# Moving the Wq preparation into the first feed-forward phase and regrouping buffers and statistics in a macaron transformer layer

## The chip, the cores and the metric

The kernel runs on one Trainium2 chip, on all eight of its cores. Every core runs the same program on its own two sequences of the batch of sixteen, and no core waits for another. The metric is the device time of the slowest core, in microseconds (us). The engines of a core are named as the profile names them: PE is TensorE's matrix multiply, PEld its weight load, DVE is VectorE, ACT is ScalarE, POOL is GpSimd and SP is SyncE. SP and POOL here do little but issue DMAs; a "q" behind an engine's name is its queue of such issues.

## The reference

The layer is a feed-forward half step, attention, and a second feed-forward half step, each ahead of a residual sum. Cut to what matters:

```python
def ln(x):  return (x - mean(x)) / sqrt(var(x) + 1e-5)      # over 1024
def ffn(x): return (silu(x @ wg.T) * (x @ wu.T)) @ wd.T     # hidden 3072, int weights / 127
def attn(x):                                                # 16 heads of 64
    xn = ln(x) * ln_g + ln_b
    q, k, v = xn @ Wq + bq, xn @ Wk + bk, xn @ Wv + bv
    return softmax(q @ k.T / 8, over the keys) @ v

x = x + 0.5 * ffn(ln(x))      # x: [16, 2048, 1024] float32
x = x + attn(x)
x = x + 0.5 * ffn(ln(x))
```

Weights are random, `ln_g` is ones and `ln_b` zeros, but the kernel computes with all of them.

## The kernel before, in words

**Phases.** The program is a chain of phases, and each phase is a block: no engine starts the next one before all engines and the phase's DMAs are done (`flush` waits for the DMAs). First two preparation phases turn the integer weights into bf16 and transpose them into DRAM. Then come, for each of the two sequences `s`, four phases: `a1` (first feed-forward, `ffn_phase`, input x, result in the DRAM tensor `x1s`), `a2` (`qkv_phase`: Q, K and V of the whole sequence, kept in SBUF), `att` (`attn_phase`, result in the DRAM tensor `x2s`) and `c` (second feed-forward, `ffn_phase` again, with `ext_stats=True`). Within a phase each engine executes its instructions strictly in the order in which the code emits them; `deps` become semaphore waits. So the order of the work is the order of the Python loops, engine by engine.

**ffn_phase.** The 2048 rows are 16 tiles `tt` of 128 rows, in two groups `g` of eight. For a group, SP loads the tiles (L379, L388), DVE sums each (L395), ACT sums its squares (L398), and after four tiles `stats_chain` (L194 to L212) turns the sums into mean and reciprocal deviation by a short ping-pong of ACT and DVE. Then, tile by tile, DVE normalises into `xntm` (L422), PE transposes (L435), DVE evacuates into `xnfm` (L444). Then 48 blocks of 16 gate and up matmuls (L483, L489) with SiLU on ACT (L500) and the product on DVE (L506); the weight slabs are loaded two ahead by SP (L461, L465). Then 16 blocks of 24 down matmuls (L527), each followed by the residual sum on DVE (L545); POOL stores a finished tile (L554). Tiles 0 to 11 use eight slots `xst`, so that tiles 8 to 11 wait until tiles 0 to 3 are summed at L545; tiles 12 to 15 have a buffer of their own, `xst2`. Phase `c` does not compute the statistics of tiles 0 to 11: the attention phase left their sums in `sm2_s` and `sm2_q`, and three chains at the phase's start finish them. It computes those of tiles 12 to 15 itself, between the two groups.

**qkv_phase.** POOL loads Wq, Wk and Wv with a cast to bf16, eight DMAs each (L582). For each of the three PE multiplies the bias of the layer norm into it (L597, 16 matmuls), DVE adds the bias vector (L607) and scales the weight by `ln_g`, the "fold" (L615, 8 instructions). Then four groups `g4` of four tiles: load (L647), sums (L652 on DVE, L655 on ACT), chain, normalise (L669), transpose (L682), evacuate (L694); 8 blocks each of Q and K (8 matmuls L714 and a bias matmul L720, evacuated at L738 through two PSUM banks) and 8 of V (L756, L762, L771).

**attn_phase.** For each of four query groups `qg` and eight head pairs `hp`: 16 rounds of two score matmuls (L960) and one exponential on ACT (L974), with the matmuls of the probabilities and V (L869) of the head pair before in between. Twice per head pair DVE normalises the result into `x2b` (L892, L897, L902), and PE may not reuse the PSUM banks before that. After the first head pair of the next query group, `drain_qg` sums four tiles of the old one with x1 (L923) and POOL stores them (L929). x1 comes into `x1q`, which holds two tiles: the load for tiles 2 and 3 (L917) waits for the first two sums, and DVE waits for this load. Later `stats_push` computes on DVE, for query groups 0 to 2, the sums that phase `c` uses (L937, L941, L944).

The lines of the phases' main loops can be followed below; the statistics chain and `drain_qg` are where the order of DVE decides.

Of the kernel before, what the change touches and what calls it, by code (L numbers as in the profile page):

```python
# [7 lines left out]
F32 = mybir.dt.float32  # L8
BF16 = mybir.dt.bfloat16
# [7 lines left out]
D = 1024  # L17
# [18 lines left out]
class Phase:  # L36
# [26 lines left out]
    def op(self, eng, fn, deps=(), inc=None, n=1, pre_nops=0, pre_drain=False,  # L63
           fdeps=()):
# [11 lines left out]
        for t in fdeps:  # L76
            if t is None:
                continue
            sem, val, ep, src = t
            if ep < p.epoch:  # L80
                continue
            wl.append((sem, val))
            if val > p.waited.get((eng, sem), -1):
                p.waited[(eng, sem)] = val
            waits.pop(sem, None) if waits.get(sem, -1) <= val else None
# [36 lines left out]
def build_program(debug=False, stages=("prep", "a1", "a2", "norm", "b", "c")):  # L122
# [51 lines left out]
    sm2_s = SB("sm2_s", [128, 16], F32)  # L174
    sm2_q = SB("sm2_q", [128, 16], F32)
    sm2_m = SB("sm2_m", [128, 16], F32)
    sm2_r = SB("sm2_r", [128, 16], F32)
# [16 lines left out]
    def stats_chain(ph, b, t_red, t_sq, prev_done, bufs=None):  # L194
        ss, qq, mm_, rr = bufs if bufs else (sm_s, sm_q, sm_m, sm_r)
        c0, c1 = b * 4, b * 4 + 4
        deps = [t_red[b * 4 + i] for i in range(4)] if t_red else []
        t_m = ph.op("scalar", lambda e: e.mul(mm_[:, c0:c1], ss[:, c0:c1], 1.0 / D),  # L198
                    deps=deps + ([prev_done] if t_red is None else []), inc="sc")
        t_m2 = ph.op("scalar", lambda e: e.activation(  # L200
            sm_t1[:, c0:c1], mm_[:, c0:c1], AF.Square),
            deps=[prev_done, t_m], inc="sc")
        t_var = ph.op("vector", lambda e: e.scalar_tensor_tensor(
            out=sm_t2[:, c0:c1], in0=qq[:, c0:c1], scalar=1.0 / D,
            in1=sm_t1[:, c0:c1], op0=ALU.mult, op1=ALU.subtract),
            deps=[t_m2] + ([t_sq[b * 4 + i] for i in range(4)] if t_sq else []),
            inc="ev")
# [4 lines left out]
            rr[:, c0:c1], sm_t1[:, c0:c1]), deps=[t_sd], inc="ev")  # L212
# [111 lines left out]
    def ffn_phase(name, src_ap, dst_ap, with_prep=False, ext_stats=False):  # L324
# [8 lines left out]
        with (  # L333
            nc.sbuf_tensor(name + "_xst", [128, nslots * 1024], F32) as xst,
            nc.sbuf_tensor(name + "_xs2", [128, 4 * 1024], F32) as xst2,
            nc.sbuf_tensor(name + "_xntm", [128, 4 * 1024], BF16) as xntm,
# [30 lines left out]
            if ext_stats:  # L367
                for b_ in range(3):
                    t_statsdone[b_] = stats_chain(
                        ph, b_, None, None,  # L370
                        t_statsdone[b_ - 1] if b_ >= 1 else None,
                        bufs=(sm2_s, sm2_q, sm2_m, sm2_r))

            for g in range(2):
                for ti in range(8):
                    tt = g * 8 + ti
                    slot = tt % nslots
                    if tt < 12:
                        t_load[tt] = ph.op("sync", lambda e, tt=tt, slot=slot: e.dma_start(  # L379
                            xst[:, slot * 1024:(slot + 1) * 1024],  # L380
                            src_ap[tt * 128:(tt + 1) * 128, :]),
                            deps=([t_xn[tt - 8],
                                   None if ext_stats else t_sq[tt - 8],
                                   t_stt.get((0, tt - 8, 1))]
                                  if tt >= 8 else []),
                            inc=ph.ld(f"x{slot}"), n=16)
                    else:
                        t_load[tt] = ph.op("sync", lambda e, tt=tt: e.dma_start(  # L388
                            xst2[:, (tt - 12) * 1024:(tt - 11) * 1024],
                            src_ap[tt * 128:(tt + 1) * 128, :]),  # L390
                            inc=ph.ld(f"y{tt - 12}"), n=16)
                    xs_ = xst2 if tt >= 12 else xst
                    xo_ = (tt - 12 if tt >= 12 else slot) * 1024
                    if not ext_stats or tt >= 12:
                        t_red[tt] = ph.op("vector", lambda e, tt=tt, xs_=xs_, xo_=xo_: e.reduce_sum(  # L395
                            sm_s[:, tt:tt + 1], xs_[:, xo_:xo_ + 1024],
                            axis=AX.X), deps=[t_load[tt]], inc="ev")
                        t_sq[tt] = ph.op("scalar", lambda e, tt=tt, xs_=xs_, xo_=xo_: e.activation(  # L398
                            sqscr[:], xs_[:, xo_:xo_ + 1024], AF.Square,
                            accum_out=sm_q[:, tt:tt + 1]),  # L400
                            deps=[t_load[tt],
                                  t_sq[tt - 1]
                                  if (tt >= 1 and (not ext_stats or tt >= 13))
                                  else None],
                            inc="sc")
                        if tt % 4 == 3:
                            b_ = tt // 4
# [713 lines left out]
```

How the kernel before makes its waits and increments, by code:

```python
                def body(e, ops=ops, eng_name=eng_name):  # L108
                    for fn, wl, inc, n, pre_nops, pre_drain in ops:
                        for sem, val in wl:
                            e.wait_ge(p.sems[sem], val)
                        if pre_drain:
                            e.drain()
                        inst = fn(e)
                        if inc is not None:
                            inst.then_inc(p.sems[inc], n)
# [5 lines left out]
def build_program(debug=False, stages=("prep", "a1", "a2", "norm", "b", "c")):  # L122
# [63 lines left out]
    def flush(ph):  # L186
        for lane in list(ph._ld.values()):
            ph.op("sync", lambda e, l=lane: e.wait_ge(sems[l], P.C[l]))
        for lane in list(ph._st.values()):
            ph.op("gpsimd", lambda e, l=lane: e.wait_ge(sems[l], P.C[l]))
        for lane in list(ph._sd.values()):
            ph.op("scalar", lambda e, l=lane: e.wait_ge(sems[l], P.C[l]))
# [893 lines left out]
                    qkv_phase(s, K_sb, Q_sb, V_sb)  # L1086
                if "b" in stages:
                    attn_phase(s, K_sb, Q_sb, V_sb)
        if "c" in stages:
            ffn_phase(f"cs{s}", x2s.ap(), out_d.ap()[s], ext_stats=True)
        if "one_seq" in stages:
            break
    ph = Phase(P, "fin")
    for i in range(8):
        ph.op("gpsimd", lambda e, l=f"st{i}": e.wait_ge(sems[l], P.C[l]))
    ph.run()
    es.close()
```

## Time and profile before

| what | value |
|---|---|
| runs of the kernel | 4415.39, 4552.08, 4901.65 us (median 4552.08) |
| the profiled execution's own time | 4441.22 us |
| its span, slowest core (core 5) | 4439.5 us; the eight cores 4383.5 to 4439.5 us |
| PE busy, share of the span | 3485.7 us, 79% |
| ACT busy | 1393.2 us, 31% |
| DVE busy | 1099.7 us, 25% |
| POOL busy | 142.8 us, 3% |
| mean granted TensorE clock, eight cores | 0.900 to 0.916 of full speed |

Shares are means over phases with different limits, so the table does not say what an edit is worth; the phases have to be read one by one. The views used are the busy time of each engine by stretch, the timeline (start in us from the span's start, duration in us, engine, line, instruction, count, and in brackets how long the engine was idle just before and who released it), the list of waits, and the list of DMA issues with the median time from issue to landing.

### The profile page before, as it was taken

To read this page: it belongs to the slowest core of one execution; us is meant where nothing else is said; L and a number is where in the kernel's file an instruction comes from. 1 tells how busy PE (TensorE), PEld (TensorE's weight loads), DVE (VectorE), ACT (ScalarE), POOL (GpSimd) and SP (SyncE) were. 2 spreads that over 40 slices of the span, in tenths; PEclk is the share of its full clock that TensorE was granted. 3 is DMA by queue.
4 is the path that set the end of the run, shared out by engine and by line. 5 is a ranking of instruction groups with operands and counts; after the bars stand their busy time and mean duration, and the time that the engine had idled before them with its cause. 6 is when DMAs were issued, how large, how long until landed. Compare 5 with 4: busy or idle time off the path is not lost. (4 is left out here: it accounts for less than half of the span.)

```text
span 4439.5 us, 57373 instructions; the slowest of 8 cores (4383.5 to 4439.5 us)
## 1 busy us (share of the span) xinstructions
PE 3485.7 (79%) x22790; PEld 1660.6 (37%) x22790; DVE 1099.7 (25%) x1734; ACT 1393.2 (31%) x1650; POOL 142.8 (3%) x267
## 2 busy tenths in 40 slices
PE   3379889678776666898996979958777676599899
PEld 2234344223233333343443434423224343344344
DVE  3421221133402212212113122123330222221221
ACT  0021111000199997111102111000029999611110
POOL 2200000100000000000000000010000000000000
PEclk9988989888889998898998989978889888899899
DMA  7933321510001110332213432150000111123220
GB/s 238 284 85 90 120 57 48 114 38 10 10 1 39 39 39 30 105 116 94 76 43 95 119 95 67 48 119 24 10 10 1 39 39 39 68 76 123 86 76 38
DMA packets 264787, 316.21 MB, mean 71 GB/s; under 512 B 9032, under 2 KB 205640, under 8 KB 263504
## 3 DMA queue, kind: packets, MB, share of 16 engines
q1 hardware_dynamic: 238288, 230.74, 17.8%
q0 software_dynamic: 26240, 81.80, 6.0%
q8 instruction: 188, 3.08, 0.3%
q14 instruction: 71, 0.58, 0.0%
HBM read 255.89 MB, written 69.21 MB: 73 GB/s over the span
## 5 line engine op out<-in xcount | busy, mean ns | idle before, releaser
L974 ACT ACTIVATE att_eS<-PS,cb 128x1024 bf16<-128x1024 f32 x1024 | 1035.2, 1190 | 47.5 <-PE PS L960 47.2
L960 PE MATMUL PS<-Q,K 64*128 64x512 bf16 x2048 | 436.3, 418 | 290.8 <-ACT att_eS L974 280.1
L869 PE MATMUL PS<-V,att_eS 128*128 128x65 bf16 x8192 | 372.4, 203 | 38.8 <-DVE att_x2b L902 38.2
L483 PE MATMUL PS<-a1s_xnfm,a1s_wslg 128*128 128x512 bf16 x1536 | 384.9, 396 | 0.0
L489 PE MATMUL PS<-a1s_xnfm,a1s_wslu 128*128 128x512 bf16 x1536 | 380.0, 392 | 0.0
L869 PEld LDWEIGHTS PS<-V,att_eS 128*128 128x128 bf16 x8192 | 309.4, 103 | 172.2 <-issue 172.2
L483 PE MATMUL PS<-cs_xnfm,cs_wslg 128*128 128x512 bf16 x1536 | 369.1, 384 | 0.0
L489 PE MATMUL PS<-cs_xnfm,cs_wslu 128*128 128x512 bf16 x1536 | 364.2, 380 | 0.0
L527 PE MATMUL PS<-cs_wdsb,cs_hsb 128*128 128x512 bf16 x1536 | 332.2, 379 | 7.5 <-DVE cs_hsb L506 7.5
L527 PE MATMUL PS<-a1s_wdsb,a1s_hsb 128*128 128x512 bf16 x1536 | 332.2, 379 | 7.5 <-DVE a1s_hsb L506 7.5
L960 PEld LDWEIGHTS PS<-Q,K 64*128 64x128 bf16 x2048 | 125.6, 94 | 492.0 <-issue 437.8
L500 ACT ACTIVATE a1s_sg<-PS 128x512 bf16<-128x512 f32 x192 | 114.6, 597 | 563.8 <-PE PS L489 563.8
L500 ACT ACTIVATE cs_sg<-PS 128x512 bf16<-128x512 f32 x192 | 114.7, 597 | 532.3 <-PE PS L489 532.3
L506 DVE TENSOR_TENSOR a1s_hsb<-PS,a1s_sg 128x512 bf16<-128x512 f32 x192 | 132.8, 692 | 571.9 <-ACT a1s_sg L500 571.9
L506 DVE TENSOR_TENSOR cs_hsb<-PS,cs_sg 128x512 bf16<-128x512 f32 x192 | 132.8, 692 | 541.1 <-ACT cs_sg L500 541.1
L483 PEld LDWEIGHTS PS<-a1s_xnfm,a1s_wslg 128*128 128x128 bf16 x1536 | 155.4, 101 | 196.4 <-issue 59.0
L489 PEld LDWEIGHTS PS<-a1s_xnfm,a1s_wslu 128*128 128x128 bf16 x1536 | 154.2, 100 | 194.4 <-issue 54.0
L892 DVE TENSOR_SCALAR att_lb<-PS 128x4 f32<-128x4 f32 x128 | 20.7, 162 | 812.9 <-PE PS L869 801.5
L527 PEld LDWEIGHTS PS<-cs_wdsb,cs_hsb 128*128 128x128 bf16 x1536 | 150.0, 98 | 189.6 <-issue 9.3
L527 PEld LDWEIGHTS PS<-a1s_wdsb,a1s_hsb 128*128 128x128 bf16 x1536 | 150.0, 98 | 189.6 <-issue 9.3
L483 PEld LDWEIGHTS PS<-cs_xnfm,cs_wslg 128*128 128x128 bf16 x1536 | 151.8, 99 | 184.1 <-issue 6.7
L489 PEld LDWEIGHTS PS<-cs_xnfm,cs_wslu 128*128 128x128 bf16 x1536 | 150.7, 98 | 183.1 <-issue 3.3
(119 smaller groups left out, 2133.7 us busy)
## 6 DMA issues: line engine op xcount, KB each, us to landing
a1s_wslg<-wgT SPq DMA_DIRECT2D x48, 512.0 KB, 4.1
a1s_wslu<-wuT SPq DMA_DIRECT2D x48, 512.0 KB, 5.4
cs_wslg<-wgT SPq DMA_DIRECT2D x48, 512.0 KB, 4.1
cs_wslu<-wuT SPq DMA_DIRECT2D x48, 512.0 KB, 5.4
x1s<-a1s_xo POOLq DMA_DIRECT2D x32, 512.0 KB, 3.0
a2s_xst<-x1s SPq DMA_DIRECT2D x32, 512.0 KB, 3.9
att_x1q<-x1s SPq DMA_DIRECT2D x16, 1024.0 KB
x2s<-att_x2o POOLq DMA_DIRECT2D x32, 512.0 KB, 4.8
```

What stands on the lines that cost most here:

```text
L483: e.matmul(gview, lg, rhs, start=(dc == 0), stop=(dc == 7))
L489: inst = e.matmul(uview, lu, rhs, start=(dc == 0), stop=(dc == 7))
L500: "scalar", lambda e, gview=gview, th=th: e.activation(sgb[:, (th % 2) * 512:(th % 2 + 1) * 512], gview, AF.Silu),
L506: "vector", lambda e, uview=uview, hc=hc, th=th: e.tensor_mul(hsb[:, hc * 1024 + th * 512: hc * 1024 + (th + 1) * 512], uview, sgb[:, (th ...
L527: inst = e.matmul(dview, hsb[:, hc * 1024 + ti * 128: hc * 1024 + (ti + 1) * 128], wdsb[:, hc * 1024 + oh * 512: hc * 1024 + (oh + 1) * 51 ...
L869: inst = e.matmul(PS1[:, (par * 2 + q2) * 512: (par * 2 + q2) * 512 + 65], expS[:, buf + kt * 1024 + par * 512 + qt * 128: buf + kt * 1024 ...
L892: t_l = ph.op("vector", lambda e, qtp=qtp: e.tensor_scalar(out=lbuf[:, qtp * 4: qtp * 4 + 4][:, :, None], in0=PS1[:, :].rearrange("p (a t) ...
L960: inst = e.matmul(PS0[:, pp + par * 512: pp + (par + 1) * 512], K_sb[64 * par:64 * par + 64, hp * 2048 + r * 128: hp * 2048 + (r + 1) * 12 ...
L974: "scalar", lambda e, hp=hp, r=r, buf=buf, pp=pp: e.activation(expS[:, buf + r * 1024: buf + (r + 1) * 1024], PS0[:, pp:pp + 1024], AF.Exp ...
```

## The change

The change has four parts. It renumbers the lines: a line L of the kernel after stands some 10 to 45 lower than its counterpart.

1. **Statistics of phase c.** `sm2_*`, `ext_stats`, `stats_push` and their three DVE instructions per tile go. Phase `c` sums all its tiles itself, as `a1` does.
2. **Buffers of ffn_phase.** `xst2` goes; tiles 12 to 15 use the eight slots and wait for tiles 4 to 7 at the residual sum. `xntm` has two buffers for four. The slabs of gate and up get semaphores of their own.
3. **Wq.** The load, bias product and fold of Wq move from `a2` to the end of `a1`, emitted behind all of a1's other work, into a buffer `wq_s` that outlives the phases. `a2` prepares Wk and Wv only. Waits for the folds are put where each weight is first used.
4. **Order in a2, buffers in att.** In `a2` the sums and the chain of group `g4+1` are emitted after the evacuations of group `g4`'s transposes, ahead of its Q, K and V. In `att`, `nsq` and `x2o` lie in `wq_s` (free by then), `x2o` has two tiles for four, and `x1q` has four tiles for two and is loaded once per query group.

```diff
@@ ffn_phase, per tile (slots are 8, tt from 0 to 15) @@
-                    if tt < 12: ... deps t_stt.get((0, tt - 8, 1)) if tt >= 8 ...
-                    else: t_load[tt] = ... xst2[...]          # no wait
-                    if not ext_stats or tt >= 12:
+                    t_load[tt] = ph.op("sync", ... xst[:, slot * 1024:(slot + 1) * 1024] ...,
+                        deps=([t_xn[tt - nslots], t_sq[tt - nslots],
+                               t_stt.get(((tt - nslots) // 8, (tt - nslots) % 8, 1))]
+                              if tt >= nslots else []),
                         t_red[tt] = ... reduce_sum
                         t_sq[tt] = ... Square
-            if ext_stats:
-                for b_ in range(3):
-                    t_statsdone[b_] = stats_chain(ph, b_, None, None, ..., bufs=(sm2_s, sm2_q, sm2_m, sm2_r))
@@ ffn_phase, after both groups (a1 only) @@
+            if wprep2 is not None:
+                wq_s, bbq = wprep2
+                for dc in range(8):
+                    wcast[dc] = ph.op("gpsimd", ... dma_start(wq_s[:, dc * 1024:(dc + 1) * 1024],
+                            Wq_d.ap()[dc * 128:(dc + 1) * 128, :]), inc=ph.st(f"w{dc % 2}"), n=16)
+                t_lb = ph.op("gpsimd", ... dma_start(bbq[0:1, :], bq_d ...))
+                t_bm = ph.op("tensor", bmm, deps=[wcast[dc] for dc in range(8)] + [t_ev[14], t_ev[15]], inc="mm")
+                ph.op("vector", ... tensor_add(bbq[0:1, :], PS0[0:1, 0:1024], bbq[0:1, :]), deps=[t_bm, t_lb])
+                for dc in range(8):
+                    ph.op("vector", ... tensor_scalar_mul(wq_s[...], wq_s[...], gch[:, dc:dc + 1]), deps=[t_bm])
             flush(ph)
@@ qkv_phase @@
-            for wi, (wsrc, wdst) in enumerate(((Wq_d, Wqs), (Wk_d, Wks), (Wv_d, Wvs))):
+            for wi, wsrc, wdst in ((1, Wk_d, Wks), (2, Wv_d, Wvs)):
...
+            emit_stats_a2(0)
             for g4 in range(4):
-                (load, sums and chain of group g4)
                 (normalise, transpose, evacuate the four tiles of g4)
+                if g4 < 3:
+                    emit_stats_a2(g4 + 1)
                 (Q, K and V of g4)
@@ attn_phase @@
+        nsq = wq_s[:, 0:4096]
+        x2o = wq_s[:, 4096:8192].bitcast(F32)
-            nc.sbuf_tensor(nm + "_x1q", [128, 2 * 1024], F32) as x1q,
+            nc.sbuf_tensor(nm + "_x1q", [128, 4 * 1024], F32) as x1q,
             def drain_qg(qg):
                 for qt in range(4):
-                    if qt == 2:
-                        t_x1[(qg, 1)] = ph.op("sync", ... x1q <- x1s tiles 2 and 3, deps=[t_x2add[(qg, 1)]])
                     t_x2add[(qg, qt)] = ph.op("vector", ... x2o = x2b + x1q,
-                        deps=[t_yev[(qg, 7, qt // 2)], t_x1[(qg, qt // 2)],
-                              t_store.get(fi - 4), t_st2.get(fi - 4)], inc="ev")
+                        deps=[t_yev[(qg, 7, qt // 2)], t_x1[qg],
+                              t_store.get(fi - 2)], inc="ev")
                     t_store[fi] = ph.op("gpsimd", ... x2s <- x2o ...)
-                    if qg >= 1 and qg - 1 < 3 and hp in (1, 2, 3, 4):
-                        stats_push(qg - 1, hp - 1)
```

How this moves the instructions, at the three places that the prediction speaks of. POOL's queue around the border of `a1` and `a2`, before (a row is one instruction or, with xN, a run of N):

```order
L554 DMA x1s<-a1s_xo 128x1024 x16
L102 UNCONDITIONAL_BRANCH
L118 UNCONDITIONAL_BRANCH
L582 DMA a2s_Wq<-L_attn_Wq 128x1024 x8
L582 DMA a2s_Wk<-L_attn_Wk 128x1024 x8
L582 DMA a2s_Wv<-L_attn_Wv 128x1024 x8
```

The same place after (`Wqh` is the buffer `wq_s`; the two branches are the border of the phases):

```order
L508 DMA x1s<-a1s_xo 128x1024 x16
L519 DMA Wqh<-L_attn_Wq 128x1024 x8
L523 DMA bbq<-L_attn_bq 1x16x64
L91 UNCONDITIONAL_BRANCH
L107 UNCONDITIONAL_BRANCH
L572 DMA a2s_Wk<-L_attn_Wk 128x1024 x8
```

The loads of Wq have moved over the border, and in POOL's queue they stand behind all 16 stores of `a1`.

DVE in `a2` from the last evacuation of group 0's transposes to the first normalisation of group 1, before (`sm_s` are the sums, `Q`, `K`, `V` the evacuations of the matmuls):

```order
L694 COPY a2s_xnfm<-PS 128x8x128
L738 CAST Q<-PS 128x512 x8
L738 CAST K<-PS 128x512 x8
L771 CAST V<-PS 128x8x64 x8
L652 TENSOR_REDUCE sm_s<-a2s_xst 128x1 x4
L203 SCALAR_TENSOR_TENSOR sm_t<-sm_q,sm_t 128x4
L211 RECIPROCAL sm_r<-sm_t 128x4
L669 TENSOR_SCALAR a2s_xntm<-a2s_xst,sm_m,sm_r 128x1024
```

The same place after:

```order
L686 COPY a2s_xnfm<-PS 128x8x128
L642 TENSOR_REDUCE sm_s<-a2s_xst 128x1 x4
L187 SCALAR_TENSOR_TENSOR sm_t<-sm_q,sm_t 128x4
L194 RECIPROCAL sm_r<-sm_t 128x4
L734 CAST Q<-PS 128x512 x8
L734 CAST K<-PS 128x512 x8
L770 CAST V<-PS 128x8x64 x8
L661 TENSOR_SCALAR a2s_xntm<-a2s_xst,sm_m,sm_r 128x1024
```

The four sums and the chain have moved from behind the 24 evacuations to ahead of them.

SP's queue in the attention phase, before (one row for each load of `x1q` until the third query group):

```order
L948 DMA att_x1q<-x1s 128x2x1024
L917 DMA att_x1q<-x1s 128x2x1024
L987 DMA att_x1q<-x1s 128x2x1024
L917 DMA att_x1q<-x1s 128x2x1024
L987 DMA att_x1q<-x1s 128x2x1024
```

The same queue after, for all four query groups:

```order
L925 DMA att_x1q<-x1s 128x4x1024
L962 DMA att_x1q<-x1s 128x4x1024 x3
```

The loads in the middle of a drain (L917) are gone; each remaining load has four tiles.

## Rows read from the trace of the kernel before

**Rows 1.** Stretches c, a1: length, PE, PEld, DVE, ACT, POOL busy, clock, DMA, GB/s

```profile
1776.00:2342.00 566.00, 517.57 (x2432) 238.53 (x2432) 117.17 (x172) 69.92 (x120) 8.52 (x16) 0.95 0.28 86
2342.00:2926.00 584.00, 516.40 (x2432) 238.32 (x2432) 130.96 (x184) 83.34 (x144) 8.52 (x16) 0.93 0.28 83
```

**Rows 2.** Timeline, start of c (sequence 0), then start of a1 (sequence 1)

```profile
1776.34 4.04 SPq L379 DMA_DIRECT2D cs_xst<-x2s  x8
...
1783.10 1.01 PE L435 MATMUL PS<-ident,cs_xntm 128*128 128x128 bf16 x8 [25.67 <-DVE cs_xntm L422]
...
2342.93 4.52 SPq L379 DMA_DIRECT2D a1s_xst<-L_attn_x  x8
...
2362.25 1.01 PE L435 MATMUL PS<-ident,a1s_xntm 128*128 128x128 bf16 x8 [25.29 <-DVE a1s_xntm L422]
```

**Rows 3.** Timeline between the two groups, in c (sequence 0), then in a1 (sequence 1)

```profile
2065.23 1.01 PE L435 MATMUL PS<-ident,cs_xntm 128*128 128x128 bf16 x8 [9.07 <-DVE cs_xntm L422]
...
2642.11 4.60 DVE L395 TENSOR_REDUCE sm_s<-a1s_xs 128x1 f32<-128x1024 f32 x4
...
2649.13 1.01 PE L435 MATMUL PS<-ident,a1s_xntm 128*128 128x128 bf16 x8 [15.06 <-DVE a1s_xntm L422]
```

**Rows 4.** DMA issues: line, count, KB each, median us from issue to landing

```profile
x1s<-a1s_xo POOLq DMA_DIRECT2D x32, 512.0 KB, 3.0
a2s_xst<-x1s SPq DMA_DIRECT2D x32, 512.0 KB, 3.9
...
x2s<-att_x2o POOLq DMA_DIRECT2D x32, 512.0 KB, 4.8
```

**Rows 5.** Timeline, border of a1 and a2, sequence 0

```profile
834.53 0.26 SPq L591 DMA_DIRECT2D a2s_bvec<-L_attn_bq  x1
835.01 4.25 POOL L582 DMA_DIRECT2D a2s_Wq<-L_attn_Wq  x8 [4.83 <-POOLq L102]
...
852.70 4.95 PE L597 MATMUL PS<-a2s_Wq,bchb 128*1 128x512 bf16 x16 [24.38 <-DMA a2s_Wq<-L_attn_Wq]
...
858.97 3.24 DVE L615 TENSOR_SCALAR a2s_Wq<-a2s_Wq,gch 128x1024 bf16<-128x1024 bf16 x8
...
864.81 5.71 PE L597 MATMUL PS<-a2s_Wk,bchb 128*1 128x512 bf16 x16 [7.16 <-DMA a2s_Wk<-L_attn_Wk]
```

**Rows 6.** Timeline of a2, sequence 0: first Q evacuation of group 0, then group 1's start

```profile
909.93 0.69 DVE L738 CAST Q<-PS 128x512 bf16<-128x512 f32 x1 [4.36 <-PE PS L720]
...
960.11 4.59 DVE L652 TENSOR_REDUCE sm_s<-a2s_xst 128x1 f32<-128x1024 f32 x4
...
966.06 0.18 DVE L211 RECIPROCAL sm_r<-sm_t 128x4 f32<-128x4 f32 x1 [0.49 <-ACT sm_t L208]
...
967.30 1.01 PE L682 MATMUL PS<-ident,a2s_xntm 128*128 128x128 bf16 x8 [7.90 <-DVE a2s_xntm L669]
...
969.98 1.01 PE L682 MATMUL PS<-ident,a2s_xntm 128*128 128x128 bf16 x8 [1.67 <-DVE a2s_xntm L669]
```

**Rows 7.** Timeline, first drain in att (sequence 0); last row: sixth stall (sequence 1)

```profile
1359.26 2.35 DVE L923 TENSOR_TENSOR att_x2o<-att_x2b,att_x1q 128x1024 f32<-128x1024 bf16 x2
...
1361.05 0.54 POOL L929 DMA_DIRECT2D x2s<-att_x2o  x1 [512.10 <-DVE att_x2o L923]
...
1373.84 3.12 ACT L974 ACTIVATE att_eS<-PS,cb 128x1024 bf16<-128x1024 f32 x3 [4.69 <-PE PS L960]
...
3742.52 4.13 ACT L974 ACTIVATE att_eS<-PS,cb 128x1024 bf16<-128x1024 f32 x4 [5.52 <-PE PS L960]
```

**Rows 8.** Waits over the whole span: us in total, times, longest us

```profile
DVE att_x2o L923 <- DMA att_x1q<-x1s: 63.6, 8, 9.6
...
ACT att_eS L974 <- PE PS L960: 47.2, 49, 7.1
```

**Rows 9.** Busy time by stretch: gate and up matmuls of group 0 in both a1

```profile
256.00:428.00 172.00, 172.00 (x653) 71.21 (x651) 28.05 (x41) 25.17 (x41) 0.00 (x0) 0.82 0.20 56
...
2382.00:2555.00 173.00, 171.07 (x787) 77.12 (x786) 33.89 (x49) 29.94 (x49) 0.00 (x0) 0.99 0.33 98
```

More of the change, by code:

```diff
@@ L75, in op @@
         wl = []
[L76 to L85, printed above, removed]
         for sem, val in waits.items():
@@ L558, in ffn_phase, with bmm @@
                         inc=ph.st(f"o{ti % 2}"), n=16)
+            if wprep2 is not None:
+                wq_s, bbq = wprep2
+                wcast = {}
+                for dc in range(8):
+                    wcast[dc] = ph.op(
+                        "gpsimd", lambda e, dc=dc: e.dma_start(
+                            wq_s[:, dc * 1024:(dc + 1) * 1024],
+                            Wq_d.ap()[dc * 128:(dc + 1) * 128, :]),
+                        inc=ph.st(f"w{dc % 2}"), n=16)
+                t_lb = ph.op("gpsimd", lambda e: e.dma_start(
+                    bbq[0:1, :], bq_d.ap().rearrange("(a d) -> a d", a=1)),
+                    inc=ph.st("bv"), n=16)
+                def bmm(e):
+                    for oi in range(2):
+                        for dc in range(8):
+                            inst = e.matmul(
+                                PS0[0:1, oi * 512:(oi + 1) * 512],
+                                bchb[:, dc:dc + 1],
+                                wq_s[:, dc * 1024 + oi * 512:
+                                     dc * 1024 + (oi + 1) * 512],
+                                start=(dc == 0), stop=(dc == 7))
+                    return inst
+                t_bm = ph.op("tensor", bmm,
+                             deps=[wcast[dc] for dc in range(8)]
+                             + [t_ev[14], t_ev[15]],
+                             inc="mm")
+                ph.op("vector", lambda e: e.tensor_add(
+                    bbq[0:1, :], PS0[0:1, 0:1024], bbq[0:1, :]),
+                    deps=[t_bm, t_lb], inc="ev")
+                for dc in range(8):
+                    ph.op("vector", lambda e, dc=dc: e.tensor_scalar_mul(
+                        wq_s[:, dc * 1024:(dc + 1) * 1024],
+                        wq_s[:, dc * 1024:(dc + 1) * 1024],
+                        gch[:, dc:dc + 1]),
+                        deps=[t_bm], inc="ev", pre_nops=1)
             flush(ph)
@@ L641, in qkv_phase, with emit_stats_a2 @@
             t_ve = {}
-            for g4 in range(4):
+            def emit_stats_a2(g4):
                 for ti in range(4):
@@ L664, in qkv_phase @@
                             t_statsdone[b_ - 1] if b_ >= 1 else None)
+            emit_stats_a2(0)
+            for g4 in range(4):
                 for ti in range(4):
@@ L847, in attn_phase @@
             t_store = {}
-            t_st2 = {}
             t_exp = {}
@@ L1068, in build_program @@
     for s in range(NSEQ):
+        es2 = ExitStack()
+        wq_s = bbq = None
+        if {"a2", "b"} & set(stages):
+            wq_s = es2.enter_context(nc.sbuf_tensor(f"Wqh{s}", [128, 8 * 1024], BF16))
+            bbq = es2.enter_context(nc.sbuf_tensor(f"bbq{s}", [1, 1024], BF16))
         if "a1" in stages:
-            ffn_phase(f"a1s{s}", x_d.ap()[s], x1s.ap())
+            ffn_phase(f"a1s{s}", x_d.ap()[s], x1s.ap(),
+                      wprep2=((wq_s, bbq) if wq_s is not None else None))
             if debug and s == 0:
```

238 lines of the change are left out of this document (92 added, 146 removed).

## The prediction

> **What bounds the kernel now.** I read the busy time by stretch first, phase by phase, because the shares of the whole span mix four kinds of phase. The reader is to see that the two feed-forward phases do the same matmuls (2432 in each, 517.57 and 516.40 us of PE) and still differ by 18 us, 566 against 584 [rows 1]: DVE and ACT are busier in `a1`, and that work stands where PE waits. So PE bounds these phases, and the ends of the matmul runs are where an edit counts. Then I read the timeline at every place where PE starts again after a pause: the bracket behind a transpose tells how long PE stood [rows 2, 3, 5, 6]. In the attention phase ACT bounds: its exponentials follow each other without a gap but for 49 waits of 47.2 us together [rows 8], and six long ones (4.30 to 7.12 us, 32.6 together, the first and the last shown) come just after the drains, when DVE has waited for x1 [rows 7, 8]. Last comes the list of issues, for what a transfer takes when it is alone [rows 4].
>
> **The change part by part.** All terms are for the whole run: two sequences, the two alike unless I say so.
>
> *Statistics in c: +37.1.* Phase `c` gets the start of `a1`. From SP's first load to the first transpose `c` takes 1783.10 − 1776.34 = 6.76 us, `a1` 2362.25 − 2342.93 = 19.32 [rows 2]; that is 12.56 more. Between the groups PE stands 9.07 us in `c` and 15.06 in `a1` [rows 3], 5.99 more. Twice 18.55 is 37.1, and the two lengths in [rows 1] (18 apart) say the same. Bounds: 33, if the loads of x2 land a little sooner than those of x, and 40. The DVE work taken out of the attention phase (`stats_push`) gives nothing back: ACT is the bound there, and its long waits are not at that place.
>
> *Buffers in ffn: 0.* The loads of tiles 12 to 15 now wait for tiles 4 to 7. The last can be issued when the last residual sum is done: PE ended at 2649.13 − 15.06 = 2634.07, the sum 0.7 later. A load alone lands 3.9 us after its issue [rows 4], at about 2638.8; DVE begins the sums of tiles 12 to 15 at 2642.11 [rows 3]. So what hides it is the four sums and the chain of tiles 8 to 11, by 3 us. The first two slabs of the second group are issued behind that load, but the first gate matmul comes only after eight transposes. If the cover were gone it would cost under 4 us at each of four places. Two `xntm` buffers suffice, because DVE alternates normalisation and evacuation and so is never a tile ahead; semaphores apart for the slabs add a wait that is long satisfied.
>
> *Wq at the end of a1: +47.7.* The loads are not hidden: in POOL's queue they stand behind all the stores, and the last store waits for the last residual sum. POOL was free of it at 835.01 − 4.83 = 830.18. From the first issue of Wq to its bias matmuls `a2` takes 852.70 − 835.01 = 17.69, and from there to the end of the fold 858.97 + 3.24 − 852.70 = 9.51 [rows 5]. So `a1`'s work ends at 830.18 + 17.69 + 9.51 = 857.4; for the border I take 1 us (bounds 0 and 1.9, which is 4.35 from 830.18 to 834.53 less the rest of a store that lands after 3.0 [rows 4]). The next phase starts at 858.4 where it started at 834.53: 23.85 late, 47.7 in all. Upper bound 49.5; lower bound 36.5, if Wq alone, with no Wk and Wv behind it in the queue, lands in the 12.11 us that Wk took after Wq.
>
> By the Trainium skill (DMA: Bandwidth & Descriptors, Specifications and Anatomy of one DMA), a core draws about 358 GB/s from HBM and a DMA has about 2.0 us of fixed cost; its estimate for the 4.19 MB of Wq is 13.7 us, against 17.69 in the row. By that estimate the sum would be 8 us lower, 4419.
>
> *a2 without Wq: −24.2.* The step from Wq's to Wk's bias matmuls, 864.81 − 852.70 = 12.11 [rows 5], falls away; Wk takes Wq's place and Wv that of Wk. Bounds: −24.2, and −16 if the loads of x1, which now start beside more of Wv's load, delay it by about one load's 3.9 us.
>
> *Order in a2: −34.4.* At each of three group borders PE stands 7.90 us before the first transpose, 1.67 before the next one [rows 6]. With sums and chain done, the first has what the next has: 6.23 gained. In exchange the sums stand before the Q evacuations. DVE is free at 909.93 − 4.36 = 905.57, sums take 4.59, the chain 966.24 − 964.70 = 1.54, so the first Q evacuation starts at 911.70 for 909.93, 1.77 late [rows 6]. PE meanwhile fills the second bank, so I take 0.5 of it (bounds 0 and 1.77). Six borders: −6 × 5.73. Bounds −37.4 and −26.8. The tiles' loads are hidden, as the slots that they wait for are normalised before; what is late next is the chain of normalise, transpose and evacuate, which stays.
>
> *Drains in att: −40.1.* DVE's eight waits for x1 (63.6 us, 7.95 each [rows 8]) go, as x1 of all four tiles is there before. In their place the third sum waits for the store of the first. That store is issued at 1361.05, 0.56 before the second sum ends at 1361.61 [rows 7]. A store lands after 3.0 us where nothing runs beside it and after 4.8 in this phase, where the 1 MB loads of x1 do [rows 4]. I take 3.5, nearer the lone one, since two stores are under way; the wait is then 2.94, and 63.6 − 8 × 2.94 = 40.1. The fourth sum finds its store landed. Bounds: −29.7 with 4.8; −43 with 3.0, where the six stalls of ACT are used up and only the two last drains, at the phase's end, give all. Behind the waiting sum on DVE stands the normalisation that PE and so ACT wait for, as before.
>
> **Sum.** 37.1 + 47.7 − 24.2 − 34.4 − 40.1 = −13.9. The profiled execution took 4441.2 us, its span 4439.5; so 4427 us. With all ends of one kind it is 4406 or 4458. The profiled time is 2.4% below the median of the runs shown (4552.08); set on that median the same sum would be 4538. A measurement of this kernel can tell about 2% (89 us) from no change.
>
> **The rivals.**
>
> *The store wait takes the load wait's place.* For it: third and fourth sum need stores to DRAM that are issued only 1.7 us before. If each wait stays 7.95 the drains give nothing: 4427 + 40 = 4467. Against it: 3.0 and 4.8 in [rows 4].
>
> *The sums ahead of Q hold PE up by what they save,* because a sum finds its tile not yet landed. Then a2's order gives nothing: 4461. Against it: the last load of a group waits for a normalisation about 7 us ahead of its sum, and lands in 3.9 [rows 4].
>
> *The change does what it seems to be for, and Wq is hidden in a1:* POOL's issues would start ahead of the last stores. Only bias matmuls, fold and border stay, about 4 us for each sequence instead of 23.85: 4388. Against it is POOL's order.
>
> *Slower, by the clock.* In the first `a1`, the gate and up matmuls of group 0 ran at a granted clock of 0.82, between the two levels, and 653 of them took 172.00 us; in the second, at 0.99, the upper level, 787 took 173.00 [rows 9]: 0.263 and 0.220 us each, 33.5 us for the 768 of a group. If the longer pauses in `c` make its four groups start like that first one, 134 us come on top: 4561. Over 2% it is only with all four; three give 4528. Against it: the second `a1` came out of pauses of 25.29 and 15.06 us [rows 2, 3], what `c` gets, and ran at 0.99.
>
> By the Trainium skill (TensorE: Matmul & The Clock Gate, Part 1, Seeing it yourself), a peak-current limit takes a die to 13/16 of the clock once three of its cores run dense matmuls. The 0.82 agrees with that figure; that all later groups on eight cores ran at 0.99 does not.
>
> **How the numbers follow.** Forecast 0.72, store wait 0.10, sums ahead of Q 0.07, hidden Wq 0.04, slower clock 0.05; 0.02 for a gain of over 2% that I cannot name. The predicted time is the forecast's, 4427. Its own bounds, 4406 to 4458, take in the ends of the unknown costs; the range runs from 4390, near the hidden Wq, to 4530, so that the first two rivals and a clock lowered in up to three groups lie inside. Faster by over 2% would be under 4352: 0.02. Slower by over 2% needs the clock: 0.05. The rest, 0.93, is within 2%.
>
> **What would show it.** Right: PE's first transpose in `c` about 19 us after SP's first load, and about 15 us of standing between the groups; the first issue of Wq right behind the last store of `a1`, its bias matmuls some 17 us later with PE idle all that time; `a2`'s first transpose about 12 us nearer to the phase's start; 1.7 us instead of 7.9 ahead of the first transpose of groups 1 to 3, with the first Q evacuation 1.8 us later; DVE waiting some 3 us for a store in each drain, and ACT's six stalls nearly gone. Wrong: a first `c` matmul stretch with a clock near 0.8, a drain wait near 8 us, sums in `a2` that wait for a load, or Wq landing while down matmuls still run.

## The result, and the profile after

| | before | after |
|---|---|---|
| median of 13 runs each | 4415.39 us | 4388.61 us |
| ratio, 95% interval | | 0.9933, 0.9915 to 0.9951 |
| the profiled execution's span, slowest core | 4439.5 us | 4381.3 us |

The change saves 0.67%, some 30 us (22 to 38), which is within 2%. The forecast was a saving of 13.9 us and a time of 4427; 4388.6 lies just below the range, which began at 4390. Single runs reach 4902 us before and 4796 us after, since some executions are disturbed; the ratio leaves those out, a median does not.

I read the trace phase by phase, on each of the eight cores, from one event of PE to the next. The table has the median over the cores of each piece between two events, summed over both sequences; "again" is a second profile of the same kernel (told of below). The first row is made of two pieces, cut at Wq's first bias matmul. With the border taken in one piece its four medians are 105.7, 107.8, 125.8 and 126.2, a change of 20.1 for the first pair of profiles and 18.4 for the second, so this row is known to some 2 us.

| PE, from ... to ... (us, both sequences) | before | again | after | again | change | forecast |
|---|---|---|---|---|---|---|
| a1's last down matmul to the end of Wv's bias product | 107.8 | 106.4 | 124.3 | 126.1 | +16.5 | +23.5 |
| a2, first transpose to last V matmul | 557.8 | 557.6 | 517.2 | 516.8 | −40.6 | −34.4 |
| from there to the first scores | 71.2 | 71.2 | 69.6 | 70.6 | −1.5 | 0 |
| att, first scores to last probability matmul | 1096.9 | 1096.7 | 1066.0 | 1063.6 | −30.9 | } |
| from there to c's first transpose | 50.9 | 50.5 | 64.6 | 64.3 | +13.7 | } −3.0 |
| c, standing between the groups | 18.1 | 18.1 | 30.2 | 30.2 | +12.0 | } |

The sum is −30.8; all other stretches together changed by under 1 us. So the time of the phases and the timed ratio agree, and the trace tells where the 30 us are.

Now the places of the prediction. The timeline of the kernel after, slowest core (core 6): start, duration, engine, line, and in brackets the idle time before and its releaser.

```profile
798.58 0.53 POOL L508 DMA_DIRECT2D x1s<-a1s_xo  x1 [9.83 <-DVE a1s_xo L498]
799.10 4.26 POOL L519 DMA_DIRECT2D Wqh<-L_attn_Wq  x8
...
817.93 5.06 PE L530 MATMUL PS<-Wqh,bchb 128*1 128x512 bf16 x16 [20.69 <-DMA Wqh<-L_attn_Wq]
...
828.27 4.26 POOL L572 DMA_DIRECT2D a2s_Wk<-L_attn_Wk  x8 [24.40 <-POOLq L91]
...
875.73 1.01 PE L674 MATMUL PS<-ident,a2s_xntm 128*128 128x128 bf16 x8 [11.66 <-DVE a2s_xntm L661]
...
885.48 4.59 DVE L642 TENSOR_REDUCE sm_s<-a2s_xst 128x1 f32<-128x1024 f32 x4
...
891.53 1.29 DVE L734 CAST Q<-PS 128x512 bf16<-128x512 f32 x2
...
941.38 0.61 PE L674 MATMUL PS<-ident,a2s_xntm 128*128 128x128 bf16 x8 [1.67 <-DVE a2s_xntm L661]
...
1321.34 2.35 DVE L914 TENSOR_TENSOR Wqh<-att_x2b,att_x1q 128x1024 f32<-128x1024 bf16 x2
...
1327.48 1.23 DVE L914 TENSOR_TENSOR Wqh<-att_x2b,att_x1q 128x1024 f32<-128x1024 bf16 x1 [3.80 <-DMA x2s<-Wqh]
...
1720.37 4.03 SPq L354 DMA_DIRECT2D cs_xst<-x2s  x8
...
1739.32 1.01 PE L391 MATMUL PS<-ident,cs_xntm 128*128 128x128 bf16 x8 [33.30 <-DVE cs_xntm L378]
...
2026.83 1.01 PE L391 MATMUL PS<-ident,cs_xntm 128*128 128x128 bf16 x8 [15.05 <-DVE cs_xntm L378]
...
2884.77 4.26 POOL L519 DMA_DIRECT2D Wqh<-L_attn_Wq  x8
...
2899.48 5.35 PE L530 MATMUL PS<-Wqh,bchb 128*1 128x512 bf16 x16 [16.56 <-DMA Wqh<-L_attn_Wq]
...
2910.09 4.26 POOL L572 DMA_DIRECT2D a2s_Wk<-L_attn_Wk  x8 [20.57 <-POOLq L91]
```

From the top: Wq is issued right behind a1's last store, and PE stands 20.69 us for it in the first sequence, 16.56 in the second (18.83 and 14.71 from the issue; 17.69 in [rows 5]). The loads of Wk start 29.17 us after the first of Wq (799.10 to 828.27), and 25.32 in the second sequence. In a2 the four sums precede the first evacuation of Q, which comes 6.05 us after the sums begin where DVE was idle 4.36 [rows 6]; the first transpose of group 1 has 1.67 us of standing before it where it had 7.90, and takes 0.61 us where it took 1.01. The third sum of a drain waits 3.80 us for a store. Phase c needs 18.95 us from its first load to its first transpose (6.76 before [rows 2]) and stands 15.05 us between the groups (9.07 [rows 3]).

The waits of the kernel after over the whole span (total, times, longest):

```profile
DVE Wqh L914 <- DMA x2s<-Wqh: 25.8, 14, 4.3
...
ACT att_eS L951 <- PE PS L937: 15.2, 37, 1.9
```

DVE's 63.6 us for x1 have become 25.8 for the stores: the eight third sums wait 2.40 to 4.28 us, 2.90 on average, and six of the eight fourth sums 0.24 to 0.76. ACT's 47.2 us, of which 32.6 lay in six long waits [rows 7, 8], have become 15.2, with none over 1.9.

### The profile page after: what moved, and what is told of

Read it like the earlier page. It is cut to its first block and busy times, and to the rows that moved or that the text cites. A ratio compares the mean times of both kernels' runs of the same rounds, so it can differ in the third digit from the quotient of the medians.

```text
span 4381.3 us, 57275 instructions; the slowest of 8 cores (4352.2 to 4381.3 us)
## 1 busy us (share of the span) xinstructions
PE 3413.2 (78%) x22558; PEld 1641.2 (37%) x22790; DVE 1045.8 (24%) x1686; ACT 1418.9 (32%) x1698; POOL 144.9 (3%) x269
## 5 line engine op out<-in xcount | busy, mean ns | idle before, releaser
L951 ACT ACTIVATE att_eS<-PS,cb 128x1024 bf16<-128x1024 f32 x1024 | 1033.7, 1201 | 15.3 <-PE PS L937 15.2
L867 PE MATMUL PS<-V,att_eS 128*128 128x65 bf16 x8192 | 362.1, 200 | 12.1 <-DVE att_x2b L900 11.7
L439 PE MATMUL PS<-a1s_xnfm,a1s_wslg 128*128 128x512 bf16 x1504 | 364.2, 382 | 2.4 <-issue 0.9
L445 PE MATMUL PS<-a1s_xnfm,a1s_wslu 128*128 128x512 bf16 x1504 | 359.9, 379 | 1.7
L867 PEld LDWEIGHTS PS<-V,att_eS 128*128 128x128 bf16 x8192 | 300.4, 102 | 139.9 <-issue 139.9
L937 PEld LDWEIGHTS PS<-Q,K 64*128 64x128 bf16 x2048 | 126.2, 94 | 499.0 <-issue 444.7
```

What stands on the lines that cost most here:

```text
L439: e.matmul(gview, lg, rhs, start=(dc == 0), stop=(dc == 7))
L445: inst = e.matmul(uview, lu, rhs, start=(dc == 0), stop=(dc == 7))
L867: inst = e.matmul(PS1[:, (par * 2 + q2) * 512: (par * 2 + q2) * 512 + 65], expS[:, buf + kt * 1024 + par * 512 + qt * 128: buf + kt * 1024 ...
L937: inst = e.matmul(PS0[:, pp + par * 512: pp + (par + 1) * 512], K_sb[64 * par:64 * par + 64, hp * 2048 + r * 128: hp * 2048 + (r + 1) * 12 ...
L951: "scalar", lambda e, hp=hp, r=r, buf=buf, pp=pp: e.activation(expS[:, buf + r * 1024: buf + (r + 1) * 1024], PS0[:, pp:pp + 1024], AF.Exp ...
```

## Experiments

**Is the base of the sum high?** The forecast was added to a profiled execution of 4441.2 us, 25.8 above the median of the runs. Busy time by stretch of that execution, the stretch of [rows 9], on core 0 and then on core 4:

```profile
256.00:428.00 172.00, 169.29 (x773) 76.90 (x787) 33.87 (x49) 29.94 (x49) 0.00 (x0) 1.00 0.34 98
...
256.00:428.00 172.00, 172.00 (x658) 71.29 (x657) 28.36 (x41) 25.75 (x43) 0.00 (x0) 0.81 0.25 70
```

Core 5 has 0.82 [rows 9]; the other five have 0.98 to 1.00, as core 0. From the first gate matmul to the first down matmul of that group 201.4 and 202.0 us pass on cores 4 and 5, and 168.5 to 170.1 on the others. Core 5 is the slowest core, so its 32 us stand in the time that I took as base. The kernel before was profiled again without an edit, and the kernel after timed again beside it:

> The kernel before, unchanged, profiled once more: was the base of my sum high? Theory (the profiled execution that I added to, 4441.2 us, was 26 us above the median of the undisturbed runs, because on cores 4 and 5 alone the first gate and up matmuls of group 0 of the first a1 ran at clock 0.81 and took 202 us for 169 to 170): the stretch takes 168 to 174 us on all eight cores, at a clock of 0.95 or more, and the slowest core's span is 4400 to 4418. Rival (the low clock belongs to the start of this program on these cores): 200 us again on two cores or more, and a span of about 4440.

> The kernel after, unchanged, timed once more on the chip of this call. Theory (by the phases of all eight cores the change takes 30 us off): a ratio to before of 0.993, and from the first transpose to the first transpose of the next phase a1 630 to 637, a2 293 to 294, att 561 to 567, c 582 to 585 on each core. Rival (the 0.9933 measured belongs to the chip it was measured on): my forecast's own sum without its base, 13.9 us, 0.997.

Kernel before, second profile, the page's first line:

```profile
span 4411.3 us, 57373 instructions; the slowest of 8 cores (4373.5 to 4411.3 us)
```

The stretch of [rows 9] in that profile, on the slowest core (core 5):

```profile
256.00:428.00 172.00, 170.08 (x781) 76.69 (x780) 33.89 (x49) 29.99 (x49) 0.00 (x0) 1.00 0.34 98
```

The stretch takes 168.4 to 170.4 us on all cores, and the span is 4411.3. The base was high by a clock that this one execution had on two cores. The rival falls, as the same kernel ran without it; that these two cores were slow in this stretch once more, in the profile of another kernel, stands in the last section. The kernel after came to 0.9959 (0.9911 to 1.0007) of before, which by itself tells neither 0.993 nor 0.997; its phases do: in the table their sum is 28.9 us below that of the second profile of before. On single cores they run past what I expected (the first a1 633 to 641, a2 to 296, att 561 to 571, the first c to 585.5).

**The order in a2 alone,** in the kernel before:

```diff
-            for g4 in range(4):
+            def emit_stats_a2(g4):
                 for ti in range(4):            # load, sums, chain of group g4
...
+            emit_stats_a2(0)
+            for g4 in range(4):
                 for ti in range(4):            # normalise, transpose, evacuate
...
+                if g4 < 3:
+                    emit_stats_a2(g4 + 1)
```

> The kernel before with one part of the change alone: in a2 the sums and the chain of the next group stand ahead of Q, K and V of this one. Theory (the order is worth more than I forecast, because two transposes of each group run at the higher clock once the pause is gone): from the first transpose of a group to that of the next 64.9 us for 71.7, 6.8 less at each of six borders, 41 us in all, a ratio of 0.991. Rival 1, the forecast's own term: 5.73 at each border, 34.4 in all, 0.992 and a step of 65.9. Rival 2, what the whole change gained in a2 came from the waits for the folds that it also moved, not from the order: step above 67, under 28 us.

Ratio 0.9907 (0.9892 to 0.9922). First transposes of groups 0 and 1 (timeline of PE):

```profile
866.50 1.01 PE L684 MATMUL PS<-ident,a2s_xntm 128*128 128x128 bf16 x8 [11.66 <-DVE a2s_xntm L671]
...
932.22 0.61 PE L684 MATMUL PS<-ident,a2s_xntm 128*128 128x128 bf16 x8 [1.66 <-DVE a2s_xntm L671]
```

The step is 65.72 here; over all cores the medians of the three steps are 65.65, 64.88 and 64.85 for 71.67, 71.58 and 71.63, and a2 is 41.4 us shorter in both sequences together. The order alone gives what the whole change gained in a2, and more than the 34.4 forecast: rival 2 falls. So does rival 1, though by the phases alone: the ratio's interval still holds its 0.992. The first border gains 6.0, the others 6.7 and 6.8.

**Is the surplus the clock?** The kernel before with matmuls that keep PE busy through the pause, read by its trace alone:

```diff
+                if g4 >= 1:
+                    def warm_fn(e):
+                        for i in range(28):
+                            inst = e.matmul(PS1[:, 1024:1536], Wks[:, 0:128], Wks[:, 512:1024], start=True, stop=True)
+                        return inst
+                    ph.op("tensor", warm_fn, inc="mm")
```

> The kernel before, with 28 matmuls of 128x512 more on PE in a2 behind the last V matmul of groups 0 to 2; their result is not used and goes to a PSUM bank that is free there. They fill 6 of the 7.9 us for which PE stands, while the order of DVE, and so the moment at which the first tile of the next group is normalised, stays as it was. Theory (the second gain of the new order is the clock: after a shorter pause the next transposes run at the upper level): the first two transposes of groups 1 to 3 take 0.61 us for eight, as in the kernel after, instead of 1.01, and from a group's first transpose to the next group's 70.8 us pass for 71.65, 0.8 to 1.0 less at each border, with the first transpose at the same time after the last V evacuation. Rival (the transposes are quicker for what DVE does then, not for PE's pause): 1.01 and 71.65 as before.

Its timeline of PE on core 0, group 0 to 1:

```profile
917.64 6.22 PE L669 MATMUL PS<-a2s_Wk 128*128 128x512 bf16 x28
925.61 0.61 PE L690 MATMUL PS<-ident,a2s_xntm 128*128 128x128 bf16 x8 [1.75 <-DVE a2s_xntm L677]
927.88 1.01 PE L690 MATMUL PS<-ident,a2s_xntm 128*128 128x128 bf16 x8 [1.67 <-DVE a2s_xntm L677]
```

Over eight cores, two sequences and three borders (48 places) the first transposes take 1.01 us in all 48 in the kernel before; with PE kept busy 46 of 48 are shorter (23 of 24 on cores 0 to 3), in the kernel after all 48. What decides for the first is PE's pause: with the order of DVE as it was, the rival falls. The second, though, takes 0.61 us in 7 places of 48 here and in 31 in the kernel after, and the step shrinks by 0.1 to 0.3 us (median of the cores at each border), not by 0.8 to 1.0. From a group's first transpose to Q's first matmul 9.98 us pass in the kernel before, 9.58 here and 9.18 in groups 2 and 3 of the kernel after (medians). So the theory is right for the first transpose, which is worth 0.40 of these 0.80 us; why the second transpose keeps the upper clock in the new order is open. The granted clock (third number from the end) of the 11.4 us from group 1's first transpose on, by stretch, core 0. Kernel before:

```profile
927.90:939.30 11.40, 5.24 (x35) 3.64 (x37) 4.93 (x7) 3.23 (x6) 0.00 (x0) 0.50 0.57 184
```

Kernel after:

```profile
928.60:940.00 11.40, 5.18 (x37) 3.28 (x39) 7.24 (x10) 2.30 (x4) 0.00 (x0) 0.64 0.55 185
```

Kernel before with PE kept busy:

```profile
925.50:936.90 11.40, 4.97 (x36) 3.41 (x38) 4.93 (x7) 3.35 (x6) 0.00 (x0) 0.54 0.55 185
```

0.50 is the lower of the two levels (1.2 GHz), and the others are a mixture with the upper. By the Trainium skill (TensorE: Matmul & The Clock Gate, Part 1) the array falls to half its clock after it has stood idle and comes back once it is busy. The first transposes agree with it: they run at the lower level in 48 of 48 places behind the pause, and in 2 of 48 with PE kept busy.

**The drains alone,** in the kernel before, with no wait for load or store:

```diff
-            nc.sbuf_tensor(nm + "_x1q", [128, 2 * 1024], F32) as x1q,
-            nc.sbuf_tensor(nm + "_x2o", [128, 4 * 1024], F32) as x2o,
+            nc.sbuf_tensor(nm + "_x1q", [128, 4 * 1024], F32) as x1q,
...
+                    xsl = x1q[:, qt * 1024:(qt + 1) * 1024]
+                        xsl, x2b[:, qt * 1024:(qt + 1) * 1024], xsl),
+                        deps=[t_yev[(qg, 7, qt // 2)], t_x1[qg]], inc="ev")
...
+                    if hp == 4 and qg > 0:      # load of x1, after the stores and stats_push
```

> The kernel before with another treatment of the drains alone: x1q has four tiles, loaded once for each query group, and the sum is written in place into x1q, so that no sum waits for a load or a store. The statistics of phase c stay in the attention phase. Theory (the drain's wait is what the attention phase loses): the six long stalls of ACT go (32.6 us) and the two drains at the end of the phase lose their wait of some 7.5 us each: 47 us less, a ratio of 0.989. Rival 1: part of what the change gained in the attention phase came from taking the statistics out of DVE, so that with them 10 us or more of the stalls stay: 37 us or less, 0.992. Rival 2: the loads of 2 MB, now issued only after the fourth head pair, come late and DVE waits for them: no gain.

Ratio 0.9911 (0.9884 to 0.9938). The four sums of a drain, in the timeline of this kernel:

```profile
1330.94 4.62 DVE L916 TENSOR_TENSOR att_x1q<-att_x2b,att_x1q 128x1024 f32<-128x1024 bf16 x4
```

What ACT still waits for, in its list of waits:

```profile
ACT att_eS L964 <- PE PS L950: 12.3, 41, 0.4
```

The attention phases are 36.0 us shorter and the stretches from there to c's first transpose 13.8: 49.8. The interval holds that (0.9887) and also rival 1's 0.992; the trace settles it, since with the statistics left in DVE no stall of ACT is over 0.4 us on this core, or 0.54 on any.

**The store wait alone:** the same sum in place, in the kernel after.

> The kernel after with one edit in the attention phase: the sum is written in place into x1q (four tiles), so that no sum waits for a store; the load for the next query group waits for the four stores. Theory (the store waits of 2.5 and 0.3 us in each drain are what is left of the drains' cost): DVE goes through the four sums in under 5 us, the two drains at the phases' ends give 2.7 each, the six in between some 0.5 to 1 each, as little of them reaches ACT: 8 to 11 us less than the kernel after, a ratio to before of 0.991. Rival 1, all eight waits of 2.7 reach the end: 22 us less, 0.988. Rival 2, the load of x1, which now waits for the stores, comes late and DVE waits for it: no gain or a loss, 0.993 or more.

Ratio 0.9944 (0.9926 to 0.9961), not to be told from the kernel after by time. The four sums take 4.62 us in one row, as above; attention is 5.3 us shorter and c's start 3.3: 8.7 in all. The second c runs 2.8 us longer there, for a reason that I did not find, and hides part of it in the time. The ratio is what rival 2 expected, but its cause is not there: the list of waits has none for a load of x1. Rival 1's 22 us fall by the phases; of DVE's 25.8 us of waits a third was paid.

**Wq back in a2,** in the kernel after (the weights' loop runs over all three again, nothing stands in a1):

> The kernel after with its third part undone: Wq is loaded, multiplied and folded in a2 again, ahead of Wk and Wv; nothing of it stands in a1. Theory, from the phases of all eight cores (last down matmul of a1 to first transpose of a2: 65.9 and 64 us before, 76.2 and 71 after): 16.5 us less than the kernel after, about 46 less than before, a ratio of 0.9895. Rival 1, my forecast of this part: 23.5 us less than after, 0.988. Rival 2, Wq's move costs nothing, as its load takes the place of waits: 0.993, the same as the kernel after.

Ratio 0.9892 (0.9877 to 0.9906). The border (timeline, slowest core):

```profile
801.67 0.53 POOL L508 DMA_DIRECT2D x1s<-a1s_xo  x1 [9.82 <-DVE a1s_xo L498]
806.75 4.26 POOL L572 DMA_DIRECT2D Wqh<-L_attn_Wq  x8 [4.55 <-POOLq L91]
...
868.04 1.01 PE L675 MATMUL PS<-ident,a2s_xntm 128*128 128x128 bf16 x8 [11.66 <-DVE a2s_xntm L662]
```

From the last store to a2's first transpose 66.37 us pass, 77.15 in the kernel after (798.58 to 875.73). By all cores the undoing gives 16.3 us, or 18.8 with the border in one piece, so this part costs 16 to 20; 23.5 was too much by the phases, though the ratio's interval holds rival 1's 0.988. Rival 2 falls.

**Wq really ahead,** in the kernel after:

```diff
+                if g == 0 and wprep2 is not None:     # ahead of group 0's down matmuls
+                        wcast[dc] = ph.op("gpsimd", ... dma_start(wq_s[...], Wq_d ...), deps=[hmul_done], ...)
...
+                if g == 1 and wprep2 is not None:     # ahead of group 1's down matmuls
+                    t_bm = ph.op("tensor", bmm, ...)  # then the sum and the fold on DVE
```

> The kernel after with the loads of Wq issued on POOL ahead of the stores of a1's first group, and the bias matmuls and the fold ahead of the last down matmuls. Theory (the third part costs what it does because POOL's queue holds the loads behind the last store): the 21.0 us between a1's last matmul and the loads of Wk that the change added go, the 16 bias matmuls stay on PE with 3.5 to 5 us: 33 us less than the kernel after, 62 less than before, a ratio of 0.986. Rival: the 4 MB load takes DMA time from the weights of the down matmuls and from the x loads of the second group, PE waits there, and at most half of it is gained: above 0.989.

Ratio 0.9853 (0.9840 to 0.9866), 35 us below the kernel after. The loads, the bias product, the last store and the border (timeline, core 5):

```profile
429.97 4.30 POOL L506 DMA_DIRECT2D Wqh<-L_attn_Wq  x8 [222.81 <-DVE a1s_hsb L462]
...
715.62 3.61 PE L472 MATMUL PS<-Wqh,bchb 128*1 128x512 bf16 x16
...
803.55 0.53 POOL L547 DMA_DIRECT2D x1s<-a1s_xo  x1 [9.83 <-DVE a1s_xo L537]
809.64 4.24 POOL L574 DMA_DIRECT2D a2s_Wk<-L_attn_Wk  x8 [5.56 <-POOLq L91]
```

The down matmuls take no longer (83.0 us a group, as before), so the rival falls: it was POOL's order that kept the loads from being hidden. By the Trainium skill (DMA: Bandwidth & Descriptors, Rules for kernel authors) a DMA is to be issued early and waited for late; the 35 us that this edit gains agree.

**The statistics back in the attention phase,** with c as before, on top of the sum in place:

> The kernel after with its first part undone on top of the sum in place: the attention phase computes the sums of tiles 0 to 11 again, and phase c, its buffers included, is that of the kernel before. Theory (this part costs what the starts of c show, 11.7 us each, and 6.0 between its groups): 35 us less than with the sum in place alone, 45 less than the kernel after, a ratio to before of 0.983. Rival: the 36 statistics instructions on DVE in each attention phase hold up the normalisations that PE and ACT wait for, 10 us or more come back in the attention phase: 0.985 or more, with an attention phase longer than with the sum in place alone.

Ratio 0.9855 (0.9833 to 0.9877), 39 us below the sum in place alone, by 0.9944. The start of c (timeline):

```profile
1714.40 4.01 SPq L616 DMA_DIRECT2D cs_xst<-x2s  x8
...
1721.14 1.01 PE L672 MATMUL PS<-ident,cs_xntm 128*128 128x128 bf16 x8 [19.07 <-DVE cs_xntm L659]
```

6.74 us for 18.95. By all cores c's starts lose 23.8 and its pauses 11.7, 35.5 together; attention is 4.3 longer, less than the rival's 10. The drains alone, which kept the statistics too, had no such 4.3 (1060.8 us against 1060.6 without them), while the kernel with all that gained, below, has 1065.2; so whether DVE's statistics cost anything is open.

**All that gained,** first with Wq only, then with Wk and Wv prepared among the Q and K blocks of the first group:

```diff
+                        if g4 == 0 and oc == 2:
+                            prep_w(pi + 1, (Wks, Wvs)[pi], (bk_d, bv_d)[pi])
+                        if g4 == 0 and 3 <= oc <= 6:
+                            for dc in (2 * (oc - 3), 2 * (oc - 3) + 1):
+                                fold_w(pi + 1, (Wks, Wvs)[pi], dc)
```

> All that gained, together: the order of a2, the sum in place, the statistics of c in the attention phase, and the loads of Wq ahead of the stores of a1's first group. Theory (the parts lie in phases of their own and add up): 45 less than the kernel after by the attention phase and c, 33 to 35 by Wq, 110 less than before, a ratio of 0.975. Rival: the parts share something (DMA, DVE or the clock) and a quarter or more is lost: above 0.981.

> As the kernel with all that gained, and in a2 the bias product and fold of Wk stand among the Q blocks of the first group and those of Wv among its K blocks, so that PE does not wait for these loads before its first transpose. Theory (what is left at the border of a1 and a2 is the wait for Wk and Wv, 40 us from the last down matmul to the end of the Wv product): the first transpose comes about 25 us after the last down matmul, as at a1's own start, for some 51; 9 us of bias matmuls come back in the first group; 16 us less for each sequence, 142 less than before in all, a ratio of 0.968. Rival: the loads of x1, which now run beside all of Wk and Wv, land late, and DVE holds up the evacuations of Q by its folds: half of it or less, above 0.971.

The first has 0.9769 (0.9749 to 0.9788), 4304.1 us; the second 0.9655 (0.9636 to 0.9674), 4254.0 us, faster than both kernels. The border in the second (timeline, core 2):

```profile
798.52 0.53 POOL L553 DMA_DIRECT2D x1s<-a1s_xo  x1 [9.83 <-DVE a1s_xo L543]
...
804.53 4.24 POOL L820 DMA_DIRECT2D a2s_Wk<-L_attn_Wk  x8 [5.48 <-POOLq L91]
...
822.15 1.01 PE L927 MATMUL PS<-ident,a2s_xntm 128*128 128x128 bf16 x8 [24.97 <-DVE a2s_xntm L914]
...
838.68 3.61 PE L836 MATMUL PS<-a2s_Wk,bchb 128*1 128x512 bf16 x16
```

a2's first transpose comes 23.63 us after the last store, where the kernel after needs 77.15, and the Wk product stands in the stream of Q with no idle time before it. The parts add up, as they lie in different phases; both rivals fall.

## Why the prediction was wrong in its time, point by point

**The base: the step that failed.** "The profiled execution took 4441.2 us [...]; so 4427 us" adds the terms to an execution whose slowest core had lost 32 us to a clock of 0.82 in one stretch. I had that row in hand [rows 9] and used it only for a rival on c, not for the sum; the lowest of the three runs shown, 4415.39, said the same. In the second profile the stretch took no more than 170.4 us on any core, and the span was 4411.3. On 4415.4 the same terms give 4401.5. The base is 25.8 of the 38.4 us by which 4427 was too high; the terms make the rest, some 13 by the medians and 17 by the phases.

**Order in a2: −34.4, mis-sized, measured −40.6** (−41.4 by itself). The idle time that goes is right: 6.23 at each border forecast, 6.24 seen. The delay of the first Q evacuation is also as read (1.7 us), but it costs PE 0.3, by group 0 (63.70 to 63.99 us), whose transposes did not change, not 0.5. What I lacked is a gain beside it: the first two transposes of groups 1 to 3 run at the upper clock in most places, 0.8 us a group. The matmuls behind them do not gain: from Q's first matmul to that of its second block 4.04 us pass in both kernels. Six times 6.24 less, 0.3 more and 0.8 less make −40.4. My bound of −37.4 had no room for it.

**Wq at the end of a1 and a2 without it: +23.5, mis-sized, measured +16.5** (20.1 with the border in one piece, 18.4 in the second pair of profiles). The mechanism is right, the loads stand behind the last store. By sequence, in one piece, the border grew by 12.8 us in the first and 7.3 in the second (11.3 and 7.1 in the second pair), where I had 11.75 for each: the size is off in the second sequence. In the first sequence 29.17 us pass from POOL's being free of that store to the loads of Wk, and my steps give 28.7 (830.18 to 858.4, and the 0.48 from a phase's start to POOL's first issue [rows 5]); in the second it is 25.32, as Wq alone lands in 14.71 us. I used the first sequence's 17.69 for both. The estimate of 13.7 us by the Trainium skill (DMA: Bandwidth & Descriptors, Specifications and Anatomy of one DMA) is below both landings here.

**Statistics in c and drains in att: −3.0, measured −5.2.** The starts and pauses of c cost 35.5 for 37.1. The drains give some 41 for 40.1: 49.8 with no wait at all, less 8.7 for the store's. The third sum's wait, taken as 2.94, is 2.90 on average; of the 25.8 us in all, for 23.5, six fourth sums have 2.7, which I had wait for nothing. A store of the drain lands after 3.3 us in the median, where I took 3.5. That 41 meets 40.1 is in part luck: my term takes each us that DVE waits as a us of time, but 49.8 of the slowest core's 63.6 us were paid before and 8.7 of its 25.8 after, so that two errors, 13.8 and 17.1, nearly cancel.

**Buffers: 0,** right; a1's pause between the groups is unchanged (15.06 and 15.05 us, median of the cores).

**The stretch before the first scores** gave 1.5 us (0.6 in the second profile) that no step named.

**The rivals.** The store wait did not take the load wait's place. The sums ahead of Q held PE 0.3 us a group, not 5.7. Wq was not hidden, though one edit hides it; that the measured 4388.6 is this rival's 4388 is chance, as the time is made of other terms. The clock did not fall in c: its gate and up stretches take 169.10 and 168.95 us for 169.24 and 168.73. The 0.93 for "within 2%" was on the right case.

## What to carry to other kernels

Before a sum is added to a profiled execution, set that execution against the fastest runs and its slowest core against the others, stretch by stretch; a stretch that only some cores have slow wants a second profile before it is put down to the kernel. A weight that "moves into the phase before" is hidden only if the queue that issues it stands ahead of that phase's last store; read the order of the issuing engine, not the place in the source. The gain of a removed pause is not the pause alone: look at the durations of the same instructions behind a short and a long pause. And the waits of an engine that does not bound a phase are not paid in full; remove one alone to see its price.

## What the runs showed of the hardware that I had not expected

In one execution two cores of a die (4 and 5) ran a stretch at clock 0.81 and 0.82, while the other two cores of the same die (6 and 7) stayed at 1.00 with the same work; in the second profile of the same kernel all eight had 0.98 to 1.00. The profile with PE kept busy shows it again, in the same stretch and on the same two cores (core 4; core 5 has 0.81, cores 6 and 7 have 1.00):

```profile
256.00:428.00 172.00, 172.00 (x651) 70.94 (x650) 28.34 (x41) 25.17 (x41) 0.00 (x0) 0.80 0.21 56
```

In its last c it is cores 6 and 7 that take 196 and 202 us for the gate and up matmuls of the second group, and cores 4 and 5 take 169. The Trainium skill (TensorE: Matmul & The Clock Gate, Part 1) has a limit of 13/16 for a whole die; the size agrees, that the whole die is taken does not hold in these stretches. What caused it is open.

And the same 16 bias matmuls take 3.61 us amid dense work, but 5.06 and 5.35 after PE stood 20.69 and 16.56 us.
